# A fused feed-forward and attention block on one core: small loads and zeros of the first pair rearranged, and the order of splits and sums in the attention

## The reference, cut to what matters

```python
w = (qw[:, None, :] >> shifts[None, :, None] & MAXQ).reshape(-1, qweight.shape[1])
z = ((qz[:, :, None] >> shifts[None, None, :] & MAXQ) + 1).reshape(qzeros.shape[0], -1)
W = (w - z[g_idx]) * scales[g_idx]             # gate, up: 512 x 1376; down: 1376 x 512
ffn(x)  = (silu(x @ Wgate) * (x @ Wup)) @ Wdown
attn(x) = softmax(q @ k.T / sqrt(128)) @ v @ Wo + bo    # q, k, v = x @ Wqkv + bqkv, 128 wide
x = x + 0.5 * ffn(layernorm(x)); x = x + attn(layernorm(x)); x = x + 0.5 * ffn(layernorm(x))
```

## Time and profile before

| what | value |
| --- | --- |
| median of 3 runs | 834.57 us (834.16 to 834.84) |
| the profiled execution's own time | 834.31 us |
| its span in the profile | 832.5 us |
| PE busy (matmul), weight load | 816.9 us (98%), 671.9 us (81%) |
| DVE, ACT, POOL busy | 493.2, 272.8, 251.2 us |
| granted TensorE clock, mean | 0.998 |

### The profile page before, as it was taken

The page is one execution under the profiler, slowest core; times in us unless marked ns, Lnnn a source line. Parts: engine busy times, 40 slices in busy tenths (PEclk is TensorE's granted clock), DMA queues, the critical chain, the costliest instruction groups (busy, mean ns, idle before and its releaser), DMA issues.

```text
span 832.5 us, 10583 instructions
## 1 busy us (share of the span) xinstructions
PE 816.9 (98%) x3944; PEld 671.9 (81%) x3944; DVE 493.2 (59%) x809; ACT 272.8 (33%) x471; POOL 251.2 (30%) x203
## 2 busy tenths in 40 slices
PE   5999999999999999999999999999999999999998
PEld 4777778878888888788888888888878888888786
DVE  7899945766554544547766785546346644443452
ACT  3333433455111111333656871121123311211221
POOL 5555614752115061303064371062411200110100
PEclk9999999999999999999999999999999999999999
DMA  5998968865754532334053159544444155444131
GB/s 157 268 347 276 311 202 286 335 254 222 277 189 140 170 133 70 105 107 152 1 178 126 39 178 373 207 139 166 126 154 154 43 197 170 133 150 153 29 102 51
DMA packets 73405, 143.04 MB, mean 172 GB/s; under 512 B 26092, under 2 KB 37028, under 8 KB 68362
## 3 DMA queue, kind: packets, MB, share of 16 engines
q1 hardware_dynamic: 66964, 131.10, 46.4%
q10 hardware_dynamic: 5526, 7.04, 2.4%
q0 software_dynamic: 864, 4.23, 1.8%
HBM read 104.30 MB, written 37.98 MB: 171 GB/s over the span
## 4 chain that ended last, share of the span: by engine, by line
PE 94%; DVE 2%; DMA 1%; POOL 1%; issue 1%; SPq 1%; ACT 1%; DVEq 0%; POOLq 0%
PE ps L811 52%; PE ps L804 38%; PE ps L822 2%; PE ps L1198 2%; DMA qs<-in_L_ffn_up_qweight 1%; DVE xn L1741 1%; SPq L561 1%; POOL wp L2213 0%; DMA zq_gu<-in_L_ffn_up_qzeros 0%; DVE stats L1718 0%; PE ps L890 0%; PE ps L1123 0%; POOL wd L2213 0%; DVE pT L1707 0%; ACT pr L1562 0%
## 5 line engine op out<-in xcount | busy, mean ns | idle before, releaser
L804 PE MATMUL ps<-blk,ring 128*128 128x512 f32 (+1 forms) x1386 | 321.2, 390 | 0.6 <-DVE u L1710 0.5
L804 PEld LDWEIGHTS ps<-blk,ring 128*128 128x128 f32 (+1 forms) x1386 | 256.5, 185 | 59.2 <-issue 1.2
L811 PE MATMUL ps<-wd,hT 128*128 128x512 f32 (+1 forms) x1056 | 251.7, 391 | 0.2
L811 PEld LDWEIGHTS ps<-wd,hT 128*128 128x128 f32 (+1 forms) x1056 | 196.9, 188 | 42.7 <-DVE h L1877 0.5
L2265 POOL TENSOR_TENSOR h<-h,u 128x512 f32<-128x512 f32 (+1 forms) x33 | 42.7, 1293 | 322.9 <-ACT h L1446 322.9
L811 PE MATMUL ps<-xT,wp 128*128 128x512 f32 x480 | 112.8, 391 | 0.2 <-POOL wp L2213 0.2
L811 PEld LDWEIGHTS ps<-xT,wp 128*128 128x128 f32 x480 | 89.8, 188 | 19.9 <-issue 0.6
L1710 DVE TENSOR_TENSOR u<-ps,p1s 128x512 f32<-128x512 f32 (+1 forms) x66 | 45.4, 687 | 97.0 <-PE ps L804 97.0
L1446 ACT ACTIVATE h<-h 128x512 f32<-128x512 f32 (+1 forms) x33 | 20.9, 632 | 177.7 <-DVE h L1710 177.7
L1710 DVE TENSOR_TENSOR h<-ps,p1s 128x512 f32<-128x512 f32 (+1 forms) x33 | 22.8, 691 | 64.3 <-PE ps L804 64.3
L1710 DVE TENSOR_TENSOR u<-ps,u 128x512 f32<-128x512 f32 (+1 forms) x66 | 45.6, 691 | 25.3 <-PE ps L804 24.3
(11 more groups left out here) (130 smaller groups left out, 887.2 us busy)
## 6 DMA issues: line engine op xcount, KB each, us to landing
ring<-wsaved SPq DMA_DIRECT2D x29, 1024.0 KB, 5.1
ring<-wsaved SPq DMA_DIRECT2D x33, 768.0 KB, 4.3
wsaved<-wp SPq DMA_DIRECT2D x10, 1024.0 KB, 5.2
stream<-xres SPq DMA_DIRECT2D x32, 256.0 KB, 2.3
xn<-stream SPq DMA_DIRECT2D x8, 1024.0 KB, 6.8
xres<-stream SPq DMA_DIRECT2D x32, 256.0 KB, 3.5
wfull<-wf ACTq DMA_DIRECT2D x20, 256.0 KB
wsaved<-wp SPq DMA_DIRECT2D x10, 512.0 KB, 4.9
```

Source lines behind the costliest of these rows:

```text
L804: mm = pe.matmul(ps[0:w, bank, :], ring[:, slot, which, a, kt, 0:w], blk[:, which, b, kt, :], start=not onto and kt == 0 and n == 0, stop= ...
L811: mm = pe.matmul(bank_ap, lhs(a), rhs(b), start=first and n == 0, stop=last and n == 2)
```

## The change

On **DVE** the unpacking of down's zeros moves from behind the statistics to behind `unpack(0)`. On **SP** the load of unit 1 moves ahead of down's indices, unit 2 ahead of the write of down's zeros, and down's scales leave SP's queue. On **POOL** the load of down's scales into `rows_d` is issued at the very start, and the four index steps move behind `w_lo(0)`. On **PE** three idle matmuls at the start and one later go, and two row tiles of x are turned ahead of `scales_zeros(0)`. On **ACT** the six small DMAs of `tab_rest` are divided: two ahead of `plain_top`, four behind the first `silu` and `w_hi(2)`. In the attention the last `ln_apply` tile of the first sequence moves behind `heads_out`; in the second sequence ACT's high part of q moves ahead of two other steps, the copies and splits of A22 alternate, those of A11 no longer do; DVE's sums and low parts of S3, S4 swap places with each other and with `total`; POOL's S1 moves up next to S2.

```diff
@@ -473,7 +473,7 @@
         FIRST_STEPS, PART_STEPS = 3, 7
-        ZERO_STEPS, ZERO_D_STEPS, TAB_STEPS = PACK + 2, 2 * PACK + 3, 2 * PACK + 4
+        ZERO_STEPS, TAB_STEPS, ZERO_D_STEPS = PACK + 2, PACK + 3, 2 * PACK + 4
@@ -522,7 +522,7 @@
...
-            return d_sz[i % 2], 16 * (i // 2 + 1)
+            return d_sz[i % 2], 16 * (i // 2 + 1 + (i + 1) % 2)
@@ -651,17 +651,16 @@
...
                 sp.dma_start(zb_gu[row:row + GK, :], zs_gu[m][m * ZP:(m + 1) * ZP, :]).then_inc(d_zb, 16)
+            load_units(sp, [1])
...
             sp.dma_start(idx_d[0:INTER - last, NT - 1:NT], g_idx[2][last:INTER].rearrange("(p o) -> p o", o=1)).then_inc(d_idx_d, 16)
-            sp.dma_start(rows_d[:, 0:HID], scales[2]).then_inc(d_rows, 16)
-            load_units(sp, [1])
+            load_units(sp, [2])
             sp.wait_ge(s_tab, ZERO_D_STEPS)
             sp.dma_start(rows_d[:, HID:D_ROW].bitcast(BF16), zb_d).then_inc(d_rows, 16)
-            load_units(sp, [2])
             load_units(sp, [3, 4, 5])
@@ -1084,13 +1083,11 @@
             pe.wait_ge(d_small, 32)
-            keep_warm(8)
-            pe.wait_ge(s_oh, 3)
-            scales_zeros(0)
+            keep_warm(5)
             for r in range(RT):
                 if r == 2:
-                    keep_warm(1)
+                    pe.wait_ge(s_oh, 3)
+                    scales_zeros(0)
                 pe.wait_ge(s_ln[0], r + 1)
@@ -1327,6 +1324,13 @@
...
+            def send_parts(n):
+                act.wait_ge(s_cut, PART_STEPS)
+                for m in range(2):
+                    row = FOLD * m + GK * n
+                    act.dma_start(tab_rest[row:row + GK, :], sc_part[n][SP_ROWS * m:SP_ROWS * (m + 1), :]).then_inc(d_cut_rest, 16)
             def w_hi(u):
@@ -1367,6 +1371,9 @@
...
                     w_hi(3 * i + 2)
+                    if i == 0:
+                        send_parts(1)
+                        send_parts(2)
                     if i == 9:
@@ -1529,12 +1536,7 @@
...
             w_hi(1)
-            act.wait_ge(s_cut, PART_STEPS)
-            for m in range(2):
-                for n in range(3):
-                    row = FOLD * m + GK * n
-                    act.dma_start(tab_rest[row:row + GK, :], sc_part[n][SP_ROWS * m:SP_ROWS * (m + 1), :]).then_inc(d_cut_rest, 16)
+            send_parts(0)
             plain_top()
@@ -1602,15 +1604,14 @@
...
                 exp(1, 2)
+                qk_hi(3, 0, qT)
                 heads_hi(1, 0)
                 exp(1, 3)
-                qk_hi(3, 0, qT)
                 p_hi(1, 2)
-                x21(2, 0)
-                x21(2, 1)
-                x_hi(2, A22, 0)
-                x_hi(2, A22, 1)
+                for kt in range(2):
+                    x21(2, kt)
+                    x_hi(2, A22, kt)
                 scaled(1, 0)
@@ -1622,8 +1623,8 @@
...
                 x_hi(2, A11, 0)
+                x_hi(2, A11, 1)
                 x11(0)
-                x_hi(2, A11, 1)
                 x11(1)
@@ -1734,10 +1735,10 @@
...
-            def ln_apply(t):
+            def ln_apply(t, tiles=range(RT)):
                 dve.wait_ge(s_rstd, deviations(t))
-                for r in range(RT):
+                for r in tiles:
                     dve.tensor_scalar(x_rows(t)[:, r, :], x_rows(t)[:, r, :], mv[:, t % 2, r, 0:1], rstd[:, t % 2, r:r + 1],
@@ -2021,8 +2022,6 @@
...
             ln_var(0, (2, 3))
-            dve.wait_ge(d_zq_d, 16)
-            unpack_zeros(dve, tables, zq_d, zi_d, (zb_d, 1.0, 1.0))
             dve.wait_ge(d_idx_gu, 32)
@@ -2033,6 +2032,8 @@
...
             unpack(0)
+            dve.wait_ge(d_zq_d, 16)
+            unpack_zeros(dve, tables, zq_d, zi_d, (zb_d, 1.0, 1.0))
             dequantise(0)
@@ -2102,10 +2103,9 @@
                 p_lo(1, 2)
-                x_sum(2, S1, 0)
-                x_sum(2, S1, 1)
-                x_lo(2, A22, 0)
-                x_lo(2, A22, 1)
+                for kt in range(2):
+                    x_sum(2, S1, kt)
+                    x_lo(2, A22, kt)
                 p_lo(1, 3)
@@ -2132,11 +2132,11 @@
...
                 inverse(1, 7)
+                sum_lo(2, S3, 0)
+                sum_lo(2, S3, 1)
                 x_sum(2, S4, 0)
+                heads_out(1, 3)
                 x_sum(2, S4, 1)
-                sum_lo(2, S3, 0)
-                heads_out(1, 3)
-                sum_lo(2, S3, 1)
@@ -2187,17 +2187,19 @@
...
                     if g == 3:
-                        ln_apply(t)
+                        ln_apply(t, (0, 1, 2))
                     heads_out(b, g)
+                    if g == 3:
+                        ln_apply(t, (3,))
                 t_lo(3, (0, 1))
             middle(NT)
+            sum_lo(2, S4, 0)
+            sum_lo(2, S4, 1)
             total(1, QT - 2)
             total(1, QT - 1)
-            sum_lo(2, S4, 0)
             up_bottom(NT)
-            sum_lo(2, S4, 1)
             gate_bottom(NT)
@@ -2280,6 +2282,8 @@
             cutter(lambda: pool.memset(zb_gu[Z_ROWS, :], Z_MARK))
+            pool.dma_start(rows_d[:, 0:HID], scales[2]).then_inc(d_sz[0], 16)
             pool.wait_ge(s_cst, 8)
@@ -2288,18 +2292,20 @@
...
             scale_parts(pool, cutter)
-            pool.wait_ge(d_idx_d, 32)
-            indices(lambda: pool.tensor_scalar(idf_d[:, :], idx_d[:, :], -float(GD), GD - 1.0, ALU.max, ALU.min))
-            indices(lambda: pool.tensor_scalar(neg_d[:, :], idf_d[:, :], 0.0, float(GD), ALU.is_lt, ALU.mult))
-            indices(lambda: pool.tensor_tensor(out=idf_d[:, :], in0=idf_d[:, :], in1=neg_d[:, :], op=ALU.add))
-            indices(lambda: pool.tensor_copy(idx_d[:, :], idf_d[:, :]))
             for u in range(UNITS):
...
                 m, i = unit(u)
+                if u == 0:
+                    pool.wait_ge(d_idx_d, 32)
+                    indices(lambda: pool.tensor_scalar(idf_d[:, :], idx_d[:, :], -float(GD), GD - 1.0, ALU.max, ALU.min))
+                    indices(lambda: pool.tensor_scalar(neg_d[:, :], idf_d[:, :], 0.0, float(GD), ALU.is_lt, ALU.mult))
+                    indices(lambda: pool.tensor_tensor(out=idf_d[:, :], in0=idf_d[:, :], in1=neg_d[:, :], op=ALU.add))
+                    indices(lambda: pool.tensor_copy(idx_d[:, :], idf_d[:, :]))
+                    pool.wait_ge(d_sz[0], 16)
+                    pool.wait_ge(d_rows, 16)
                 if u < 2:
-                    pool.wait_ge(d_rows, 32)
                     gather(u)
@@ -2342,12 +2348,10 @@
                         add_bias(b, [j - 2 + RT])
-                    if b and j == RT + 1:
-                        for kt in range(2):
-                            sum_lo(2, S1, kt)
                     if b and j == RT - 1:
-                        for kt in range(2):
-                            sum_lo(2, S2, kt)
+                        for what in (S2, S1):
+                            for kt in range(2):
+                                sum_lo(2, what, kt)
             pair(2)
...
             pair(3)
```

## The result

The changed kernel took **839.89 us** (median; 837.33 to 841.16 over 6 runs) against 834.52 (834.16 to 835.23) for the kernel before beside it: ratio 1.0058, 95% interval 1.0047 to 1.0069. It is slower by 5.4 us. I had forecast 834.0 with a range up to 836.4. The profiled execution took 841.16, span 839.3, mean granted clock 0.994; before it was 834.31, 832.5 and 0.998.

A forecast was written before the change was run, and what follows sets the result against it. The ending chain was taken as 94% PE's own work, so time could come only from the start (+0.4) and the attention (-1.0). That gave -0.6 from the 834.57 median: 834.0 us, own range 832.8 to 835.4, widened to 832.1 to 836.4.

The forecast's parts named there:

- Zeros, POOL and the meter: Start: zeros and POOL steps run later, but the meter (`silu` times up, tile 0; gate product, tile 2) stays unchanged.
- My +0.4 for this part: Start: first gather, issued at 19.9, lands at 27.0 against DVE's use at 26.7; +0.4 us, ends 0 and +0.6.
- The six small DMAs: Start: four issued from about 22.9 to 25.5 on ACT land in time for tile 2's scales; no cost.
- The far end of my bound: Start: the last four small DMAs take 6.6 us to land, as before; the near end was within 3 us.
- rival A: Start: late small DMAs delay tile 2's scales to 32.1; start +2.9, total +1.9, 836.5; chance 0.15.
- B: Start: lower clock holds through tile 0's gate product, taking 5.4 us, not 2.7; total +1.0, 835.6; chance 0.15.
- The attention's gains: Attention: PE waits at 437.33, 467.19 and 471.47 go, -0.4 and -1.0, with A11 costing +0.4; sum -1.0 us.
- `heads_out`: Attention, first sequence: PE's projection no longer waits for DVE's `heads_out`, one normalised tile now behind it; -0.4 us.
- q and A22: Attention, second sequence: earlier q high part and alternating A22 copies and splits remove two PE waits; -1.0 us.
- A11: Attention: copy `x11(0)` becomes ACT's third step, 0.48 us later, delaying DVE's low part and PE's score; +0.4 us.
- The end: Attention's end: a PE wait goes but POOL's S1 delays the last bias addition; 0 us (-0.6 to +0.5).

The follow-up runs named there:

- experiment 10: `start_rest`: the changed kernel with the six small DMAs together ahead of `plain_top` and DVE's and POOL's end order as before; 833.11 us.
- experiment 1: `parts_first`: the changed kernel with all six small DMAs ahead of `plain_top` again, as before; 834.73 us.
- experiment 4: `split_parts`: the kernel before with only the small DMAs divided, two ahead of `plain_top`, four behind the first `w_hi(2)`; 835.59 us.
- experiment 6: `late_gathers`: the kernel before with the small DMAs divided and each of the first two gathers issued one unit later; 837.54 us.
- experiment 11: `zeros_late`: the kernel before with only the unpacking of down's zeros moved behind `unpack(0)` on DVE; 836.37 us.
- Experiment 5: `warm_gaps`: the changed kernel with idle matmuls in PE's two gaps, 14 ahead of the scales of tile 2, 9 ahead of product 4; 837.28 us.
- Experiment 3: `gains_only`: the kernel before with only the last `ln_apply` tile behind `heads_out`, q's high part ahead and A22's alternation; 832.66 us.
- experiment 9: `gains_a11`: the kernel before with the three attention gains (`ln_apply` tile, q's high part, A22) plus ACT's new order for A11; 833.65 us.
- experiment 12: `gains_parts_sooner`: the kernel before with the three attention gains, plus three small DMAs sent ahead of `w_hi(0)` and three behind `w_hi(1)`; 833.45 us.
- experiment 8: `gains_dve_order`: the kernel before with the three attention gains plus DVE's new order at the end, POOL's S1 as before; 834.02 us.
- experiment 7: `s1_early`: the kernel before with only POOL's low parts of S1 moved right behind those of S2; 834.49 us.
- experiment 2: `old_end`: the changed kernel with DVE's and POOL's order at the end of the attention as before; 837.02 us.

## Why the prediction was wrong, point by point

**Zeros, POOL and the meter: right in place, about a microsecond short.** `dequantise(0)` came at 14.91 (forecast 14.9), `w_lo(0)` at 17.12 (17.07), `w_lo(1)` at 22.06 (21.3), `silu` times up at 26.46 (25.5). The missing 0.8 is in one row: POOL idled 0.91 ahead of the first gather, which I had not priced. That experiment 10 starts at 114.59 shows that all of this is covered. My +0.4 for this part can't be told from nothing (-0.2 there, +0.63 in experiment 1, while equal starts differ by 1.0). Its reason did not show: I had DVE wait for the first gather, and DVE goes on at 27.58 without a wait; so if the number is near, that is luck.

**The six small DMAs: this step failed, by a term put at 0 that measured some 5 us.** I wrote "I take no cost, since they then had two full copies of 256 KB in front of them on ACT's queue and the gathers beside them, and now one copy." I had moved the gathers two paragraphs earlier, to 19.9 and later, and did not carry that to this step: the small DMAs do not leave the gathers behind, they meet them. Measured, they take some 3.5 us with the gathers at 17.20 and 20.95 (experiment 4) and 6.54 with the gathers at 21.30 and 25.05 (experiment 6); the later gathers are the only edit between the two, and each has one profiled execution. In the changed kernel it was 6.84, or 6.3 from the end of the issue to the scales, as I had counted the 6.6. The far end of my bound was nearly the right value, and rival A, which I gave 0.15, was the right mechanism. I leaned on the Trainium skill's rule that the engines take turns between queues packet by packet ("DMA: Bandwidth & Descriptors", queues, rings and completion order), from which I had a short queue get through sooner. The trace doesn't bear out that inference: with a DMA share of 1.03 in the window the small DMAs took 6.8 us. (The queue was not quite short: a full copy of 256 KB went out on it at 23.52, right ahead of them, but so it did in experiment 4, at 22.57, where they took 3.5.) The row of before, 6.6 us under a full load, was the better evidence.

**The price of rival A was too low too, by the clock.** I had +2.9 for the start and measured +5.5 in the profiled execution. The scales came at 32.80, 0.7 after my 32.1. Most of the rest is the lower clock behind the gap, 1.6 us by the 9.29 and the 7.70 for the same 33 matmuls. I treated the clock as a rival of its own (B), at another gap. There it happened too. Where the small DMAs go early it is covered, as I had thought: in `parts_first` the gate product of tile 0 ran at 0.50 and the start was only +0.63. In the changed kernel it is not. I had asked only what PE waits for behind that product, `w_lo(1)`, and that did end at 23.35; but `silu` waits for the product as well, and the four small DMAs stand behind it on ACT. The product ended at 23.48 where I had 21.5, and the first of the four left at 23.89 where I had 22.9 (22.94 in experiment 4). No run has this microsecond by itself. What I also missed is that other gaps may bring the lower clock, so that a term that opens a gap can have a second one: 1.6 in the changed kernel, 1.7 in experiment 11, 2.7 in experiment 6. Experiment 5 measures it for both gaps of the changed kernel together: -2.6.

**The attention's gains: right.** -0.56 for `heads_out` (forecast -0.4), -1.06 for q and A22 (-1.0), +0.48 for A11 (+0.4). Together that is -1.1 where I had -1.0. Experiment 3 even gives 0.6 more, since the wait for `u`, which I had put down to the other edits, is gone there as well; in experiments 9 and 12, with the same three moves, it is back (0.3 and 0.6), so this part is not sure.

**The end: the step failed in size.** I had the last bias addition end at 498.9 with S2 beginning at 488.41, 10.5 us later; it ended 11.4 later (504.18 after 492.78). I had half a microsecond of hindrance in all, and in the rows one total and two bias additions take 1.74 or 1.75 in place of 1.28. The chain behind it was as I wrote (ACT's high part, DVE's low part, two totals, then the sum), and PE went on 3.5 us after the last bias addition, where I had 3.2. I had thus forecast a wait of 0.9 (502.1 against 501.2), which just eats the wait that goes; with 0.9 and 0.3 more it became 1.98. By cause: DVE's order costs 1.4 on top of the gains (experiment 8, by another collision), POOL's S1 on the kernel before nothing (experiment 7), both together 1.6 (experiments 1 and 10), and 2.9 where the clock drops behind the gap (experiment 2 against the changed kernel). The Trainium skill's rule on the shared port pair ("SBUF — State Buffer", two separate sides) agrees with the rows: DVE's subtraction with both inputs in SBUF takes 1.5 us beside POOL's and 0.68 alone (504.94). I had used it for half a microsecond in all. In the changed kernel it is DVE's two low parts of S3 (2.96 us from 497.11) and the first of S4 that stand beside POOL's totals and bias additions, and each of three POOL steps gets 0.45 longer.

**The chances.** The result lies beyond the upper end of the range, 836.4, on the side to which I had given 0.17. The cases were treated as exclusive: A, B and the end each had their own time, but here a late load, a lower clock and a late end came in one execution, and they add. The range was also summed wrongly: the bounds of its terms give 832.4 to 835.2, not 832.8 to 835.4. That changes nothing here.

What stays open: why the same wait of 1.98 us at the end is followed by the lower clock in the changed kernel and not in `parts_first`; whether SP's new order alone makes the zeros' move free; how much of the start the lower clock ahead of the small DMAs costs; and why the executions of one kernel differ by up to 6 us where the small DMAs are late (834.83 to 840.65 in experiment 6).

## What to carry to other kernels

When a change moves two things on different queues, price each at the place where the other one now is: the divided loads cost 1 us alone and the later gathers nothing (experiment 10), both together 3 us (experiment 6) to 5 (experiment 1 against the changed kernel, part of it the clock at the end). A small load that an engine needs soon is worth sending early, and if the trace has one landing time for it under a full load, take that and not the hope that it will be shorter. Give a new gap of TensorE a second price, the matmuls behind it at the lower clock (1.6 to 2.7 us here), and follow that price on every engine that waits for those matmuls, not on TensorE alone. Where a gap can't be closed, try idle matmuls in it: here they were worth 2.6 us.

## What the runs showed of the hardware that was not expected

- The landing time of the same four small DMAs (issued within 0.4 us of the same moment) nearly doubled, from some 3.5 to 6.54 us, with two gathers issued 4 us later on another queue (one profiled execution each; the medians are 2 us apart).
- Both gaps of the changed kernel, 3.21 and 1.98 us, were followed by some 3.3 us at the lower level of the clock, 1.6 us lost each. In `parts_first` the gap of 1.98 was not. In experiment 6 a gap of 3.77 was followed by 33 matmuls that lost 2.7, in experiment 11 gaps of 1.4 and less by a loss of 1.7.
- The runs of the changed kernel spread over 3.8 us (837.33 with a mean clock of 0.998, 841.16 with 0.994), while those of `warm_gaps` spread over 1.3. The fastest of the changed kernel took what `warm_gaps` takes.
- Idle matmuls in two gaps gave back 2.6 us, with the scales of tile 2 no sooner (33.06 against 32.80).
- The recorded clock can miss a slow stretch: in `warm_gaps` 24 matmuls took 8.52 us in place of 5.45 while the mean granted clock is given as 1.000.
